# Moving the ScalarE half of the probability-transpose evictions to VectorE in a fused attention and feed-forward kernel

## The reference, cut to what matters

```python
xn = _layernorm(x, axis=-1)
x = x + attn(xn, Wq, Wk, Wv, Wo) + ffn(xn, W1, b1, phases, w_real, w_imag, W2, b2)

def attn(x, Wq, Wk, Wv, Wo):          # d_k = 128, one head, causal
    Q = x @ Wq; K = x @ Wk; V = x @ Wv
    logits = einsum('bqd,bkd->bqk', Q, K) * 128 ** (-0.5)
    attn = softmax(where(causal, -inf, logits))
    return einsum('bqk,bkd->bqd', attn, V) @ Wo

def ffn(x, ...):                      # 1024 -> 4096 -> 1024
    hidden = einsum('bsd,df->bsf', x, W1) + b1
    imag = w_imag * sin(theta + hidden * 0.1)
    phase = cos(theta) * w_real + sin(theta) * w_imag
    return einsum('bsf,fd->bsd', relu(hidden + phase * imag * 0.1), W2) + b2
```

## Time and profile before

| what | value |
|---|---|
| median of 2 runs | 1247.5 us (1245.55 to 1249.46) |
| profiled execution | 1251.96 us |
| its span on the slowest core (core 6) | 1250.3 us |
| spans of the eight cores | 1241.3 to 1250.3 us |
| busy on core 6, share of the span | PE 87%, DVE 34%, ACT 49%, POOL 3% |
| attention stage, sequence 0 and 1 | about 74 to 149 us and 209 to 288 us |
| feed-forward stage | 289 us to the end |

### The profile page before, as it was taken

How to read it: one execution, slowest core, us unless ns; L and a number is a source line. 1 busy time by engine, 2 the same in 40 slices (tenths; PEclk the granted TensorE clock), 3 DMA queues, 4 the chain that set the end, 5 groups by cost and what they waited for, 6 DMA issues and landing times.

```text
span 1250.3 us, 23705 instructions; the slowest of 8 cores (1241.3 to 1250.3 us)
## 1 busy us (share of the span) xinstructions
PE 1089.8 (87%) x7810; PEld 740.6 (59%) x7936; DVE 427.7 (34%) x967; ACT 614.0 (49%) x1325; POOL 37.0 (3%) x48
## 2 busy tenths in 40 slices
PE   1757465668999999999999999999999999999997
PEld 1644364446666666666666566656666666566665
DVE  2612263422333333333333333333333333333333
ACT  2955477564545444444445454545454545454444
POOL 1310023000000000000000000000000000000000
PEclk9965778568999999999999999999999999999999
DMA  7879186941020202021120202020202020202010
GB/s 155 254 135 169 54 263 138 176 81 68 1 85 1 85 1 85 8 78 42 45 67 19 85 1 85 1 85 1 85 1 85 1 85 1 85 1 85 13 39 35
DMA packets 47416, 87.13 MB, mean 70 GB/s; under 512 B 7106, under 2 KB 23490, under 8 KB 46274
## 3 DMA queue, kind: packets, MB, share of 16 engines
q1 hardware_dynamic: 36226, 59.39, 15.0%
q0 software_dynamic: 11072, 26.22, 11.4%
HBM read 78.25 MB, written 25.17 MB: 83 GB/s over the span
## 4 chain that ended last, share of the span: by engine, by line
PE 71%; issue 2%; DVEq 2%; DVE 2%; ACT 1%; ACTq 0%
PE psOut L843 35%; PE psW L817 35%; DVEq L763 2%; DVE probs L765 1%; ACT rb_sb L790 1%; DVE u_sb L742 1%; DVE out_sb L765 0%; PE psOut L833 0%; DVEq L741 0%; DVEq L770 0%; ACT rb_sb L795 0%; ACT ss_sb L782 0%; DVEq L762 0%; DVEq L739 0%; ACTq L789 0%
## 5 line engine op out<-in xcount | busy, mean ns | idle before, releaser
L817 PE MATMUL psW<-xn_r,W_sb 128*128 128x256 bf16 x4096 | 538.8, 275 | 1.9 <-PEq L385 1.9
L843 PE MATMUL psOut<-W_sb,rb_sb 128*128 128x512 bf16 x1936 | 515.4, 383 | 17.1 <-ACT rb_sb L790 10.2
L817 PEld LDWEIGHTS psW<-xn_r,W_sb 128*128 128x128 bf16 x4096 | 404.7, 99 | 162.8 <-issue 6.7
L782 ACT ACTIVATE ss_sb<-psW,phb_sb 128x256 bf16<-128x256 f32 x512 | 241.9, 473 | 445.7 <-PE psW L817 445.7
L742 DVE SCALAR_TENSOR_TENSOR u_sb<-ss_sb,Rp_sb,psW 128x256 f32<-128x256 bf16 x512 | 244.3, 480 | 586.7 <-ACT ss_sb L782 575.4
L843 PEld LDWEIGHTS psOut<-W_sb,rb_sb 128*128 128x128 bf16 x2048 | 200.8, 99 | 151.5 <-issue 20.7
L790 ACT ACTIVATE rb_sb<-u_sb,b_sb 128x256 bf16<-128x256 f32 x511 | 254.5, 498 | 57.2 <-DVE u_sb L742 55.2
L525 PE MATMUL psT<-diag_li,xn_rg 128*128 128x128 bf16 x272 | 35.2, 286 | 20.8 <-DVE diag_li L580 11.0
L369 PE MATMUL psTx<-diag_li,probs 128*128 128x128 bf16 x176 | 15.3, 237 | 42.1 <-DVE diag_li L274 42.1
L626 ACT CAST pT_big<-psT 128x512 bf16<-128x512 f32 (+2 forms) x40 | 21.7, 542 | 54.2 <-PE psT L525 54.1
L539 PE MATMUL psO<-pT_big,V_tm 128*128 128x128 bf16 x272 | 33.1, 288 | 12.1 <-ACT pT_big L626 7.4
(11 more groups left out here) (93 smaller groups left out, 437.9 us busy)
## 6 DMA issues: line engine op xcount, KB each, us to landing
x_sb<-x SPq DMA_DIRECT2D x52, 512.0 KB, 5.7
W_sb<-w POOLq DMA_DIRECT2D x8, 2048.0 KB, 40.7
xn_scr<-xn_rg POOLq DMA_DIRECT2D x32, 256.0 KB, 4.4
xn_r<-xn_scr SPq DMA_DIRECT2D x16, 512.0 KB, 6.8
out<-out_sb SPq DMA_DIRECT2D x32, 256.0 KB, 2.2
out<-probs SPq DMA_DIRECT2D x32, 256.0 KB, 4.9
xn_r<-x SPq DMA_DIRECT2D x12, 512.0 KB, 6.4
Q_fm<-b2rep SPq DMA_DIRECT2D x1, 512.0 KB, 3.5
```

What stands on the lines that cost most here:

```text
L782: ssc3.inc(sc.activation(ss_sb[ci % 2][:], psW1[slot][:], AF.Sin, scale=0.1, bias=phb_sb[:, c:c + 1]))
L817: ins = t.matmul(psW1[slot][:], W1_sb[:, k * DFF + c * 128: k * DFF + (c + 1) * 128], xn_r3[g % 2][:, k * R3:(k + 1) * R3], start=(k == 0) ...
L843: ins = t.matmul(psOut[tt][:, h * 512:(h + 1) * 512], rb_sb[cw % 3][:, tt * 128:(tt + 1) * 128], W2_sb[:, cc * D + h * 512: cc * D + (h + ...
```

## The change

The loop in ScalarE's program that evicts bank 0 is removed. VectorE's loop, which skipped the segments of bank 0, now takes every segment of the tile in order, reads the bank that the segment lies in, and raises st2e for bank 0 and st2eV for bank 1, so PE's waits stay as they were. A wait for the segment's transposes, a wait for P·V of the tile before and a drain stand ahead of each eviction on VectorE, as they did for bank 1.

```diff
                         for si in range(nsg[j]):
-                            if bank_of[(j, si)] != 1:
-                                continue
+                            b = bank_of[(j, si)]
                             v.wait_ge(stx2.h, stx2_b + cum_sg[j] + si + 1)
                             if j >= 1:
                                 v.wait_ge(spv.h, spv_b + j)
                             v.drain()
                             w = segw2(j, si)
-                            st2eV.inc(v.tensor_copy(
+                            (st2e if b == 0 else st2eV).inc(v.tensor_copy(
                                 pT_big[si // 2][:, (si % 2) * 512:(si % 2) * 512 + w],
-                                psT2[1][:, 0:w]))
+                                psT2[b][:, 0:w]))
...
-                        if j >= 0:
-                            for si in range(nsg[j]):
-                                if bank_of[(j, si)] != 0:
-                                    continue
-                                sc.wait_ge(stx2.h, stx2_b + cum_sg[j] + si + 1)
-                                if j >= 1:
-                                    sc.wait_ge(spv.h, spv_b + j)
-                                w = segw2(j, si)
-                                st2e.inc(sc.copy(
-                                    pT_big[si // 2][:, (si % 2) * 512:(si % 2) * 512 + w],
-                                    psT2[0][:, 0:w]))
```

## The result

The changed kernel takes 1228.36 us (median of 11 runs, from 1225.82), the kernel before 1247.97 us in the same calls (10 runs). The ratio is 0.9839, 95% interval 0.9828 to 0.985: 1.6% faster, about 20 us, where 13 were forecast. The time lies inside the forecast range of 1224 to 1244.

A forecast was written before the change was run, and what follows sets the result against it. Exp of the next tile was taken to wait behind ScalarE's evictions in its queue. Gains of 7.5 (sequence 0), 4 (sequence 1) and 2 us (clock) made 13.5, rounded to 13: 1234.5 us, range 1224 to 1244.

The forecast's parts named there:

- The working of a tile at 1.2 GHz: Attention tiles step by step: late transposes 5.95 us apart instead of 6.30; sequence 0 takes 62.9 us against 69.8.
- The clock, 2 us: Attention stages: clock stays mostly at 1.2 GHz; effect between a cost of 4 and a gain of 20, taken as 2 us.
- the forecast's list: Gains by tile in sequence 0, from 1.6 us at tile 14 to a loss of 0.35 at tile 15; difference 6.9.
- the 0.1 that I had named as a sign against the forecast: Attention stage: the forecast is wrong if the granted clock moves by more than 0.1.
- Rival B: Denser attention stage is granted the full clock: 1226 us with half of the 20 us, 1216 with all; chance 0.13.
- 7.5 us in sequence 0: Attention stage of sequence 0: Exp overlapping the previous tile's work saves 6.9 us by the steps, taken as 7.5.
- 4 us in sequence 1: Attention stage of sequence 1: 72.9 becomes 69.2 us, taken as 4 us gained, with 2.1 lost to phase constants.
- VectorE's serial queue: Evictions one behind another on VectorE: a 0.08 us gap between two, costing 0.47 us in tile 14.
- the mark I had set as a sign of error: Attention tiles: the forecast is wrong if P·V waits for evictions by more than 1 us in a tile.
- Rival C: VectorE's serial evictions and constants ahead of the diagonal eat the gain, 7 us a sequence: 1246 us; chance 0.18.
- Rival D: Exp behind the o_fm copy closes a longer loop, 8.3 instead of 6.3 us a late tile: 1276 us; chance 0.03.
- a gate by the W2 load: End of attention: W2 load might gate the stage; set aside, DMA share 0.07 from 264 on, new end near 283.

The follow-up runs named there:

- e1: Kernel before, with ScalarE keeping its bank 0 evictions but behind Exp of the next tile instead of ahead of it; 1235.69 us, ratio 0.9898.
- e8: Kernel before, with useless 128-column matmuls added where PE waits and nothing else; 1249.32 us, ratio 1.0006.
- e2: Changed kernel, with VectorE's phase constants of sequence 1 placed between the diagonal and the evictions; 1222.21 us, ratio 0.9794.
- e4: Changed kernel without the drain ahead of each VectorE eviction; 1221.98 us, ratio 0.9787.
- e3: Changed kernel, with the last segment of every tile from 8 on evicted by ScalarE behind Exp; 1226.57 us, ratio 0.9819.
- f1: Changed kernel with the edits of e2, e3 and e4 together; 1216.61 us, ratio 0.9749.
- e5: Changed kernel, with useless 128-column matmuls ahead of each tile's P·V and each later segment's transposes; 1221.7 us, ratio 0.9794.
- e6: Changed kernel, with the W1 load moved out of sequence 0 and issued together with W2 in sequence 1; 1266.87 us, one run.
- g1: f1 with two of the four W2 load pieces issued inside the projection stage of sequence 1; 1232.31 us, ratio 0.9872.

## Why the prediction was right, and where it was off

**What bounds the kernel, and what goes.** Right. Exp waited for ScalarE's evictions by place and not by data. e1 gives some 60% of the gain by moving them without changing their engine, and e8 and the tiles at two levels show that PE's speed bound a tile of the old order only to a small part.

**The working of a tile at 1.2 GHz.** Right, tile by tile. On core 6 tiles 0 to 9 of sequence 0 ran at 0.50 in both kernels. Tiles 0, 2, 4 and 8, from their first transposes to the next tile's, became 0.65, 0.81, 0.58 and 1.01 us shorter where the forecast had 0.6, 0.7, 0.5 and 0.9; tiles 1 and 3 changed by less than 0.05 and tile 15 lost 0.36, where it had nothing and a loss of 0.35. The hand-overs are those of the earlier trace rows: in tile 15 VectorE starts 0.81 us after the transposes (129.36 to 130.17), two evictions take 1.47, so they stand 0.78 apart, and PE goes on 0.15 after the first (130.17 + 0.69 to 131.01).

**The clock, 2 us.** This is the term that was mis-sized. The same tiles of core 6, summed:

| tiles of sequence 0 | before | after | gain | gain by the forecast's list | PEclk before | PEclk after |
|---|---|---|---|---|---|---|
| 0 to 9 | 36.4 | 32.6 | 3.8 | about 4 | 0.50 | 0.50 |
| 10 to 14 | 30.5 | 21.7 | 8.8 | about 3 | 0.50 to 1.00 | 0.90 to 1.00 |

The steps had priced tile 13 at 5.95 us with matmuls at the lower level, and compared it with 6.30 us in the old trace, where the earlier trace rows show eight transposes in 0.61 us, the upper level. It took 4.62. A warm stretch was worth 0 to 0.6 us a tile to the old order, so little was lost by counting it cold there; in the new order it is worth more. To this came that on core 6 the upper level began at 108 us instead of 125. Sequence 0, worked at 62.9 all cold and 51.5 all warm, took 59.1 on core 6 and 56.6 on the fastest, which makes 4 to 6 us for the clock in this sequence, an estimate from these four numbers; no run holds the clock at one level. The granted clock of 74 to 124 moved by 0.16, more than the 0.1 that I had named as a sign against the forecast; it was one. Rival B, a denser stage at a higher clock, came about in part.

**7.5 us in sequence 0.** The stage lost 12.2 us on core 6 and 11.5 to 14.8 on the others. That 7.5 of it is the overlap and the rest the clock fits the tiles above, but was not measured apart.

**4 us in sequence 1.** Measured 3.9 on core 6 and about 5.6 elsewhere. The total was near by two errors that cancel, which is luck. The constants cost more than the 2.1 us put down for them: on core 6 tiles 0 to 6, all at 0.50, take 25.5 us in sequence 1 and 19.3 in sequence 0, 6.2 more, where the kernel before has 23.5 and 21.8, 1.7 more. So 4.5 us were lost, and taking the constants off the path (e2) shortened the stage by 5.8 as a mean over the cores. I had counted five tiles at 0.4 us; it is all seven, at 0.4 to 1.4 each. On the other side the late tiles gained more than worked, being at the upper level again: tiles 12 to 14 had 0.99 to 1.00, 1.00 and 0.91 to 1.00 on seven of the eight cores. Tile 10, which was to fall from 7.1 to 5.0 behind the table loads, fell to 5.6.

**VectorE's serial queue.** The 0.47 us of tile 14 and the gap of 0.08 were costed at nothing else than what the tile working gave. PE did wait for VectorE by up to 1.1 us at a time, 15.9 us in sequence 0, slightly above the mark I had set as a sign of error. e4 shows that these waits are on the path (6.5 us), and the stages of e3 agree (3.2 and 1.4 us). Rival C named the right mechanism; what it said would eat the gain ate a part that the tile working had already in it.

**Rival D.** Did not occur: ScalarE has 26.7 us of idle time in front of its o_fm copies in sequence 0, and PE's longest waits for an Exp, 2.0 us in sequence 0 and 3.6 in sequence 1, stand once each and are in the kernel before too. The price put on rival D had a slip: 8.3 less 6.3 is 2.0 us a tile and not 1.8, so 16 tiles make 32 us and not 29.

**W2.** The forecast had written off a gate by the W2 load because its share was 0.07 from 264 on. At this change's size that held (1.5 us of wait). It stopped holding some 11 us further down, in f1.

## What to carry to other kernels

Before you move work off an engine, ask whether it is in the way by its length or by its place in the queue: putting it behind the instruction that the next tile needs gave some 60% of the gain here for no transfer of work. When you compare a worked tile with one from a trace, price both at the clock level at which that tile will run, and ask which of the two orders can use a faster clock at all. And each time a stage gets shorter, look at what was hidden under it: three local gains of 14.6 us gave 11.2, and moving the load that had come to light cost more than it freed. A filler that costs time of its own cannot tell alone what a clock is worth; the same tile on cores at different levels can.

## What the runs showed of the hardware that was not expected

- Matmuls without any use, six of 128 columns a tile and three a segment, made a kernel 5 to 6 us faster where PE was on the critical path (e5), changed the time by nothing where ScalarE's queue set most of it (e8), and raised the granted clock in both (mean over sequence 0's stage 0.91 to 0.94 and 0.83 to 0.89).
- The same tile at the upper instead of the lower level took 0.7 to 0.9 us less in the new order (4.25 to 3.54, 4.97 to 4.05) and 0 to 0.6 less in the old (6.52 to 5.92 at the most).
- A PE busy 6.98 of 8 us stayed at 0.51 with a DMA share of 0.01 (e6), so neither busy time alone nor the load explains the level.
- A drain written ahead of a PSUM eviction on VectorE costs 0.12 us at each hand-over (2.90 against 2.55 us for four), 6.5 us in all over 80 evictions.
- 4 MB of weights placed inside a stage that passes its data through DMA made the way between the attention stages some 20 us longer (g1), though the share of the DMA engines there had been 0.47 in one stretch of 10 us.
